# Third layer of a four-layer image network: the leftover filter rows of two pixel groups on the two row halves of TensorE's array, with a new order of the small steps

## The reference

```
hidden = conv1x1(x, w_hidden, b_hidden)                  # 48 -> 288 channels
qkv = conv3x3_depthwise(hidden, w_dw, b_dw)              # 288 channels
q, k, v = split(qkv, 3)                                  # 96 channels each
...
out = irfft2(rfft2(q_patch) * rfft2(k_patch))            # in patches of 8 x 8 pixels
...
normed = (out - mean over channels) / sqrt(var + eps) * gamma + beta
return conv1x1(v * normed, w_out, b_out)                 # 96 -> 48
```

## Time and profile before

| | us |
|---|---|
| three executions | 16599.63, 16603.31, 16604.81 |
| median | 16603.31 |
| profiled execution, its own time | 16606.54 |
| its span, first to last instruction | 16604.7 |
| mean granted TensorE clock of the span | 0.978 of full speed |
| filter matmuls of the third layer, first and last | 5746.8 to 11873.1 |

### The profile page before, as it was taken

The page is one execution under the profiler, slowest core; times in us unless marked ns, Lnnn a source line. Parts: engine busy times, 40 slices in busy tenths (PEclk is TensorE's granted clock), DMA queues, the critical chain, the costliest instruction groups (busy, mean ns, idle before and its releaser), DMA issues. The chain is left out here.

```text
span 16604.7 us, 329530 instructions
## 1 busy us (share of the span) xinstructions
PE 15941.3 (96%) x125334; PEld 11026.7 (66%) x125334; DVE 7088.9 (43%) x15967; ACT 5712.5 (34%) x11355; POOL 2285.8 (14%) x1770
## 2 busy tenths in 40 slices
PE   7999999999899899999999999999899999999999
PEld 7876333677677655555555555555578777877787
DVE  0001333333354443444344334443456665666666
ACT  0000111212233333333333333333345554555554
POOL 0000000000004400000000000000133333333333
PEclk9999999999999999999999999999999999999999
DMA  1333666846548744444444444443211111111111
GB/s 56 135 133 116 159 159 159 154 92 153 130 145 214 167 50 49 52 50 48 52 49 50 52 50 49 52 50 49 58 35 35 37 35 37 37 37 37 34 36 35
DMA packets 2203209, 1297.30 MB, mean 78 GB/s; under 512 B 1852970, under 2 KB 2102127, under 8 KB 2108739
## 3 DMA queue, kind: packets, MB, share of 16 engines
q1 hardware_dynamic: 1934436, 1171.81, 36.6%
q10 hardware_dynamic: 267232, 104.65, 2.7%
HBM read 692.31 MB, written 450.74 MB: 69 GB/s over the span
## 5 line engine op out<-in xcount | busy, mean ns | idle before, releaser
L1470 PE MATMUL l_c<-l_wa,l_xa 128*128 128x288 f32 x12288 | 3494.0, 421 | 62.3 <-issue 62.3
L1470 PEld LDWEIGHTS l_c<-l_wa,l_xa 128*128 128x128 f32 x12288 | 2176.0, 190 | 1459.2 <-ACT l_qkv L1554 950.1
L1554 ACT ACTIVATE l_qkv<-l_c 128x288 f32<-128x288 f32 x2048 | 844.1, 412 | 3538.5 <-PE l_c L1472 3538.5
L1946 PE MATMUL l_a<-l_y,l_d 64*100 64x64 f32 x19008 | 1831.1, 255 | 112.2 <-DVE l_turn L2011 65.9
L1946 PEld LDWEIGHTS l_a<-l_y,l_d 64*100 64x100 f32 x19008 | 1782.9, 171 | 158.6 <-issue 126.7
L1946 PE MATMUL l_b<-l_y,l_d 64*100 64x64 f32 x19008 | 1837.8, 255 | 3.9 <-issue 3.8
L1946 PEld LDWEIGHTS l_b<-l_y,l_d 64*100 64x100 f32 x19008 | 1783.5, 171 | 5.5 <-issue 5.2
L1641 DVE TENSOR_TENSOR l_z<-l_f,l_ks 94x384 f32<-94x384 f32 x1024 | 567.0, 554 | 2358.9 <-ACT l_ks L1559 2358.8
L1221 PE MATMUL l1h_ps<-l1h_ring,l1h_w 96*96 96x256 f32 x6120 | 1327.2, 379 | 50.6 <-ACT l1h_ring L1169 47.0
L992 PE MATMUL l1v_ps<-l1v_rows,l1v_w 96*96 96x256 f32 x6120 | 1326.8, 378 | 31.7 <-ACT l1v_rows L965 31.7
L1472 PE MATMUL l_c<-l_wb,l_xb 96*128 96x288 f32 x4096 | 1336.5, 407 | 0.0
(11 more groups left out here) (214 smaller groups left out, 20000.8 us busy)
## 6 DMA issues: line engine op xcount, KB each, us to landing
l0a_x<-x_px_dram SPq DMA_DIRECT2D x128, 1176.0 KB, 5.1
l0b_T<-x_in_dram SPq DMA_DIRECT2D x256, 435.4 KB
l_xa<-x_dram SPq DMA_DIRECT2D x1280, 48.0 KB, 3.9
l_x<-x3p_dram SPq DMA_DIRECT2D x132, 384.0 KB
l_out<-x_dram SPq DMA_DIRECT2D x132, 384.0 KB
out_dram<-l_out SPq DMA_DIRECT2D x66, 768.0 KB, 4.3
x_dram<-l0b_out ACTq DMA_DIRECT2D x256, 193.5 KB, 5.7
x1b_dram<-l0b_out_b ACTq DMA_DIRECT2D x256, 192.0 KB, 5.7
```

The costliest lines, as they stand in the source:

```text
L1470: nc.tensor.matmul(bank[m % 2][:, 0:OUTC], xa[:, k, row * PW + x0 + dx:row * PW + x0 + dx + 128], wa[:, b, dx, :], start=(dx == 0), stop=F ...
L1554: nc.scalar.activation(qkv[:, j % 4, m, :], bank[m % 2][:, 0:OUTC], ACT.Copy).then_inc(conv_out, 1)
L1946: last = nc.tensor.matmul(bank[0:PPOS, i * 2 * TX:(i + 1) * 2 * TX], d[k, c, :], y[k, c, :], start=True, stop=True, skip_group_check=True)
```

## The change

`xb` gets 128 partitions: the 57 leftover rows stand there twice, at partitions 0 to 56 with the left 128 pixels of each image row, and at 64 to 120 with the right 128 pixels. `filters(r)` now does two neighbouring pixel groups: six matmuls on the whole array, three into each bank, and then two matmuls of 57 rows, one on the upper and one on the lower half of the array's rows, each into its own bank. The copies to `xb` are two times three copies of 18 channels x 8 rows x 128 pixels (pieces of 512 bytes) and two loads of the bias rows, where it was three copies of whole rows and one load. The zeroing of `xb` is gone. `read_conv` waits until both groups are done. The order of the steps on TensorE, ScalarE and VectorE is changed; `moments(0)` and `deviation(0)` move to the start of the next turn.

```diff
@@ window_rows
-    return a + b + [(None, None, None)] * (C2 - len(b))
+    b += [(None, None, None)] * (HI - len(b))
+    return a + b + b
@@ stage_l2
-    KB = 96
+    KB = 128
     LEFT = 15
     LAST = C - 2 * LEFT
+    TAIL = 3 * LAST + 3
-        xa, xb = sb("xa", [128, BUF, AROWS * PW]), sb("xb", [KB, 2, R * PW])
+        xa, xb = sb("xa", [128, BUF, AROWS * PW]), sb("xb", [KB, 2, R, 128])
@@ gpsimd, sync
-            nc.gpsimd.memset(xb[:], 0.0).then_inc(zeroed, 1)
-            sp.wait_ge(zeroed, 2)
+            sp.wait_ge(zeroed, 1)
@@ copy_rows
-                for dx in range(3):
-                    sp.dma_start(xb[dx * LAST:(dx + 1) * LAST, k % 2, 0:R * PW - dx],
-                                 xa[HI + 2 * LEFT:HI + C, k, PW + dx:AROWS * PW]).then_inc(spread[k], 16)
+                for h in range(2):
+                    for dx in range(3):
+                        sp.dma_start(xb[h * HI + dx * LAST:h * HI + (dx + 1) * LAST, k % 2],
+                                     xa[HI + 2 * LEFT:HI + C, k, :].rearrange("p (r w) -> p r w", w=PW)
+                                     [:, 1:AROWS, h * 128 + dx:h * 128 + dx + 128]).then_inc(spread[k], 16)
+                    sp.dma_start(xb[h * HI + 3 * LAST:h * HI + TAIL, k % 2],
+                                 D["k_inside"][1:4, bass.ds(blk * R, R), h * 128:(h + 1) * 128]).then_inc(spread[k], 16)
-                sp.dma_start(xb[3 * LAST:3 * LAST + 3, k % 2, :], rows2(D["k_inside"][1:4, bass.ds(blk * R, R), :]))\
-                  .then_inc(spread[k], 16)
@@ tensor
-            def filters(p, j, b, m):
-
-                if m == 0 and j % 2 == 0:
-                    pe.wait_ge(spread[j // 2 % BUF], (p + (PAIRS - j)) * 16)
-                pe.wait_ge(conv_out, 8 * p + (m + 1))
-                k, row, x0 = j // 2 % BUF, j % 2 * 4 + m // 4 + m % 4 // 2 * 2, m % 2 * 128
-                for dx in range(3):
-                    nc.tensor.matmul(bank[m % 2][:, 0:OUTC], xa[:, k, row * PW + x0 + dx:row * PW + x0 + dx + 128],
-                                     wa[:, b, dx, :], start=(dx == 0), stop=False)
-                nc.tensor.matmul(bank[m % 2][:, 0:OUTC], xb[:, k % 2, row * PW + x0:row * PW + x0 + 128], wb[:, b, :],
-                                 start=False, stop=True).then_inc(conv_done, 1)
+            def filters(p, j, b, r):
+
+                if r == 0 and j % 2 == 0:
+                    pe.wait_ge(spread[j // 2 % BUF], (p + (PAIRS - j)) * 24)
+                k, row = j // 2 % BUF, j % 2 * 4 + r // 2 + r % 2 * 2
+                for h in range(2):
+                    pe.wait_ge(conv_out, 8 * p + (2 * r + h + 1))
+                    for dx in range(3):
+                        nc.tensor.matmul(bank[h][:, 0:OUTC], xa[:, k, row * PW + h * 128 + dx:row * PW + h * 128 + dx + 128],
+                                         wa[:, b, dx, :], start=(dx == 0), stop=False)
+                for h in range(2):
+                    part = slice(h * HI, h * HI + TAIL)
+                    nc.tensor.matmul(bank[h][:, 0:OUTC], xb[part, k % 2, row, :], wb[part, b, :], start=False, stop=True)\
+                        .then_inc(conv_done, 1)
@@ scalar
-                act.wait_ge(conv_done, 8 * p + m + 1)
+                act.wait_ge(conv_done, 8 * p + (m // 2 * 2 + 2))
```

More of the change, by code:

```diff
@@ L128, in shape_constants @@
     c["k_diag"], c["k_sel0"], c["k_e1a"], c["k_e2a"] = diag, sel0, ea[0], ea[1]
-    ei = np.zeros((2, C + 1, 128 + C2), np.float32)
+    ei = np.zeros((2, C + 1, 256), np.float32)
     for p, (ch, _, _) in enumerate(window_rows()):
@@ L254, in lay_out @@
     w = i["L2_conv_w_dw"][:, 0]
-    dwa, dwb, bdw = (np.zeros(n, np.float32) for n in ((128, 3, C6), (C2, C6), (128, C6)))
+    dwa, dwb, bdw = (np.zeros(n, np.float32) for n in ((128, 3, C6), (128, C6), (128, C6)))
     for p, (ch, dy, dx) in enumerate(window_rows()):
@@ L1516, in turn @@
                     spectrum(p - 1, j - 1, 3)
+                if last:
+                    project(p - 2, j - 2)
                 if now:
                     filters(p, j, b, 1)
+                    spectrum(p, j, 0)
                 if before:
@@ L1522, in turn @@
                     filters(p, j, b, 2)
+                    spectrum(p, j, 1)
                 if before:
@@ L1526, in turn @@
                     filters(p, j, b, 3)
[L1527 to L1534, removed]
+                    spectrum(p, j, 2)
                     inverse(p, 0)
-                    filters(p, j, b, 7)
-                    spectrum(p, j, 2)
                 if before:
@@ L1580, in turn @@
                 now, before, _ = (there(p, n) for n in range(3))
+                if before:
+                    deviation(p - 1, 0)
                 if now:
                     read_conv(p, j, 0)
+                    read_conv(p, j, 1)
                 if before:
@@ L1586, in turn @@
                 if now:
-                    read_conv(p, j, 1)
                     read_conv(p, j, 2)
+                    read_conv(p, j, 3)
+                    read_k(p, 0)
                 if before:
                     deviation(p - 1, 1)
[L1591 to L1598, removed]
                 if now:
@@ L1602, in turn @@
                     read_k(p, 1)
+                if before:
+                    read_turned(p - 1, j - 1, 0)
+                    normalise(p - 1, 1)
+                if now:
                     read_conv(p, j, 6)
                     read_conv(p, j, 7)
-                    deviation(p, 0)
                     read_k(p, 2)
@@ L1702, in turn @@
                 if before:
+                    moments(p - 1, 0)
                     scales(p - 1, 0)
                     products(p - 1, 3)
+                if last:
+                    residual(p - 2, j - 2)
+                if before:
                     times_v(p - 1, j - 1, 0)
-                    moments(p - 1, 1)
-                    scales(p - 1, 1)
                 if now:
@@ L1710, in turn @@
                 if before:
-                    times_v(p - 1, j - 1, 1)
+                    moments(p - 1, 1)
+                    scales(p - 1, 1)
                 if last:
-                    residual(p - 2, j - 2)
+                    count(p - 2, j - 2)
                 if now:
                     products(p, 1)
-                    moments(p, 0)
+                if before:
+                    times_v(p - 1, j - 1, 1)
+                if now:
                     products(p, 2)
-                if last:
-                    count(p - 2, j - 2)
                 if isinstance(p, int) and p % (NBLK * 2) == 2 and p > 2:
```

## The result

The kernel after takes 15979.2 us (median of 4, 15976.4 to 15997.3), the kernel before 16601.5 beside it: a ratio of 0.963, 95% interval 0.961 to 0.964. Forecast were 15970 us and a range of 15860 to 16150.

The account below looks back on a forecast made before the run. TensorE was taken to bound the kernel, awaiting nothing inside a turn: 256 turns x 2.48 us = 635 saved, 16606.5 - 635 + 2 = 15973.5 for the profiled execution, 15970 us for the median; range 15860 to 16150.

Parts of the forecast that it names:

- the sum of its steps: TensorE's turn in the third layer's filters: 21.13 us after against 23.61 before, as no step awaits anything.
- 2 x 0.242 + 0.105: Price of a tail (four 57-row matmuls, two overlapped pairs): two filter streams plus first weight load, 0.585 us.
- the 105 us of the direct switches: Row-half to column-half switches on TensorE, three a turn: if free, 105 us less, 15865; if double, 16040.
- Rival 1: Leftover-row matmuls: the two halves don't overlap, 497 us come back, 16467 us; chance 0.07.
- Rival 2: Second pair of each tail and the spectrum behind pay their weight loads: 0.70 a turn, 179 us, 16149; chance 0.08.
- The split of the 2.48: Saving per turn on TensorE: 1.96 us from overlap, 0.52 from fewer switches (14 to 11) and fewer bare first loads.
- The margins: ScalarE's bank reads behind each tail finish before the next filters want the bank; smallest margin 0.6 us, no stall.
- Rival 3: New order stalls TensorE because ScalarE's times are off: say 0.5 us a turn, 128 us, 16098; chance 0.12.
- Transfers: Copies to xb in 512-byte pieces: copies and stores take 16 to 41 us, may take 42.3; hidden, cost 0.
- rival 4: Copies in 512-byte pieces land later than 42.3 us, the block's first filter waits: 16610 or more; chance 0.04.
- Start: Before the first filter: four more copy issues, and xb's zeroing was hidden anyway; about +2 us once.

Follow-up runs that it names:

- the kernel with one switch more: Kernel after, with the transpositions T0 put between the third tail (the 57-row matmuls) and spectrum 1: 16125.0 us, ratio 0.971 to the kernel before.
- the order alone: Kernel after, with the leftover rows as two 96-row matmuls on the whole array, one per pixel group, new order kept: 16433.4 us, ratio 0.990 to the kernel before.
- half the time taken away: Kernel after, with each block's copies held back until half of the next block is filtered, 21 us later: 16015.2 us, ratio 0.965 to the kernel before.
- the repeated one: Kernels after and before, both unchanged, profiled once more: 15976.0 and 16606.1 us.

## Why the prediction was right

**The bound.** TensorE awaited nothing inside a turn, so the sum of its steps was the time. It held: 21.13 forecast, 21.12 measured. Two slips in the working are small: 2 x 0.242 + 0.105 is 0.589 and not 0.585, which makes the sum 21.15, and the 105 us of the direct switches are 107.5.

**The overlap.** Rival 1 (no overlap) would have been the kernel with both tails on one half, 23.03; the tail's two starts in one instant show it wrong.

**Loads under a running half.** Rival 2 is wrong too: tail and `spectrum` follow at 0.59 and 0.74, where bare loads would have given 0.69 and 0.82. The sentence of the Trainium skill that stood behind it ("TensorE: Matmul & The Clock Gate", Part 3, The mechanism) does not hold here.

**Switches and bare loads.** In the kernel with one switch more the tail and the transpositions grew by 0.10 and 0.09 (the two switches), `spectrum` and the filters by 0.08 and 0.10 (their bare loads), as forecast term by term. The direct switch between row and column halves, the unknown of the range, costs what others cost: `spectrum` ahead of the projection takes 0.74, and 0.75 ahead of the transpositions, and the projection 1.01 as ever. That fits the drain at a change of mode that the Trainium skill has in "TensorEngine Tiling (Array Packing)", Tiling Modes, Key Properties. The split of the 2.48 was told in an uneven way: 1.96 "overlap" and 0.52 for fewer switches. By experiment the order alone gives 0.66 and the half-array tails 1.83, since the tail brings its own bare load and spares that of `spectrum`. The sum does not change.

**Waits.** The margins were 0.03 to 0.13 us smaller than worked out, as ScalarE starts its reads up to 0.12 later; with reads tripled the stall came where it was expected. Rival 3 is wrong.

**Transfers.** Hidden, as costed; rival 4 is wrong even with half the time taken away. Copies and stores of one block, from the first copy at 8186.80 until the engines fall idle near 8202 (slices of 1.175 us from 8173), took 16 us, the lower end of the 16 to 41 forecast.

**Start.** +2 us was forecast, and the first filter came 1.3 us earlier in the first pair of traces, 12.3 in the repeated one (5735.4 against 5747.7). A small miss of sign, within what the layers ahead vary by.

**The rest of the program.** I took its time as unchanged. It grew by 18 us in the profile and by 22 to 26 against the repeated ones, with TensorE longer at its lower clock: the step that was missing, 3% of the gain, and more than the 9 us between forecast and median.

**How much of the close hit is luck.** 15973.5 was forecast for the profiled execution and 15977.8 measured, but the 4.3 us are what is left of three misses: the stretch shrank by 645.8 and not 635 (10.8 in its favour), the start came 1.3 earlier and not 2 later (3.3 in its favour), and the rest grew by 18.4. The turn was right by its mechanism; that the whole came within 5 us was not.

What sets the length of a jump's gap is open; transfers don't explain it. That it is the place of the instructions in memory fits, but no run moved the instructions and nothing else. The fourth layer's time goes with the granted clock in it; what lowers the clock there more in one kernel or execution than in another is open too.

## What to carry to other kernels

Where one engine is busy throughout, list its steps with their start-to-start prices, the price of each change of mode and each bare load among them, and work out the new order's sum; then check that what others must do in between fits under it, margin by margin. Steps in one mode belong side by side. And look beyond the part that was changed: before an edit of tens of us is judged by the whole time, compare untouched stretches too, with the granted clock in each.

## What the runs showed of the hardware that was not expected

- A matmul for a free half can start ahead of an earlier one for the other half: `spectrum`'s record at 8008.95, the tail's last at 8009.19, though the tail stands first in the program. The Trainium skill, "TensorE: Matmul & The Clock Gate", Part 3, The mechanism, has matmuls start strictly in order; the rows here differ.
- A stall of 0.30 us cost 0.40: the twelve filter records behind it took 3.11 and not 3.01.
- A jump of the hardware loop left TensorE idle for 1.6 to 4.1 us in the mean, by kernel, with the DMA engines at 0.01 as well as at 0.93. Behind 11 of the 24 jumps of the kernel after, the clock was lowered: here the twelve filter records that take 3.01 took 8149.36 - 8144.57 = 4.79, at a granted clock of 0.64 over 8144.6 to 8149.4, a mean between its two levels of 1.2 and 2.4 GHz, after 2.24 us without a matmul:

```profile
8144.57 4.86 PE L1474 MATMUL l_c<-l_wa,l_xa 128*128 128x288 f32 x12 [2.24 <-issue]
8149.36 0.76 PE L1478 MATMUL l_c<-l_wb,l_xb 57*128 57x288 f32 x4
```

- Code that was not touched ran between 4727 and 4780 us, in twelve kernels, and with it went the time that TensorE spent at its lower clock there, 400 to 495 us.
